# A selective-scan and expert-mixture layer: stores of the preparation in another order, square ahead of logarithm, earlier first tiles, two accumulators

## The chip, the cores and the metric

The kernel runs on one core of a Trainium2 chip. The core has five engines with a queue each: TensorE (PE; its weight loads are listed as PEld), VectorE (DVE), ScalarE (ACT), GpSimd (POOL) and SyncE (SP), which here only starts transfers. All transfers run on the core's 16 DMA engines. The metric is the device time in microseconds of one execution; the median of several runs counts.

## The reference, cut to what matters

The input is 8 batches of 512 tokens of width 128. After a layer norm, two things are added to the input: a two-way Mamba block (16 states, 256 channels, forward and backward) and a mixture of 16 experts of which each token takes 4.

```python
xn = layernorm(x)
xz = einsum('ed,bld->bel', in_proj_w, xn);  x_, z = split(xz)
# for each direction:
u = silu(causal_conv(x_, conv_w) + conv_b)              # 4 taps
x_dbl = einsum('bdl,kd->bkl', u, xproj_w)               # rank 8, B (16), C (16)
delta = softplus(dtproj_w @ x_dbl[:, :8] + dt_bias)
dA = exp(delta * A);  dBx = delta * B * u
h = scan(h = dA * h + dBx)                              # along the 512 tokens
y = (einsum('bdln,bnl->bdl', h, C) + D * u) * silu(z)
mamba = out_proj(y_forward + y_backward)
# experts:
logits = -|xn - keys|^2 + rw @ xn + rb;  top 4, softmax -> w
ffn = sum over 4 of w * (gelu(xn @ w1[e] + b1[e]) @ w2[e] + b2[e])
out = x + mamba + ffn
```

## The kernel before, in words

Everything is hand-scheduled: each engine has one program, and semaphores order them. There are three stages.

**Start (about the first 50 us).** Input and constants are loaded, the layer norm and the routing are computed, and a slot in a table sorted by expert is worked out for each of the 4096 x 4 (token, expert) pairs (`pos`, ready in two parts). SP meanwhile fills `slots_d`, the table in device memory, with rows of zeros, and `acc_d`, the accumulator in device memory, with a copy of the input.

**Preparation (one `prepare(b)` for each of 8 batches).** On each engine the batches follow one another.
- ACT: copies `xdbl` and `part1` out of PSUM (L852, L853), takes the absolute value of the delta projection (L859), loads the table of exponential and logarithm (L861), `Exp` of minus it into `mag` (L863), `part2` (L865), the skip term (L868), logarithm of 1 + `mag` (L874), square of `small` into `fit` (L876), x of batch b+2 (L832), `parts_p` (L881), another table load and SiLU of the convolution to `u` of batch b+1 (L846), SiLU of z of batch b+2 into `zg` (L837).
- DVE: the convolution of batch b+1 (`convolve`, L1371 the first tap, L1376 three more, each tap four instructions), `small` = min(`mag`, 1/32) (L1393), the polynomial from `fit` and `small` (L1398), the larger of it and the logarithm (L1404), delta (L1411), delta times u (`du_p`, L1417). L1398 waits for the square.
- SP: stores what is ready to device memory (`store_prepared`: `c_d`, skip, parts, delta, gate, du), each as soon as its turn in SP's order comes and its source is ready.
- PE: the projections; the delta projection (L1097) uses 9 rows of `xdbl` and of `dtw`.
- POOL: beside all this, 128 indirect scatters (L750, one for each 128 rows and choice k) of the normalised tokens into `slots_d`, in four rounds of 32. Ahead of each round it waits until the last one has landed and copies a column of gates (L746).

**Scan.** For each batch, 32 pairs q = 0 to 31 (16 states in twos by 4 channel blocks). For each pair PE fills PSUM with B (L1220 or L1223), DVE multiplies (`dbx`, L1467) and scans twice (L1479), ACT makes the decays (L990), POOL multiplies with C (L783; some pairs DVE, L1487), and PE sums into PSUM four pairs later (L1159, `SUM_LAG`). Rings of 8 buffers hold decays and states. Between these, a table of events lets the expert tiles of 256 rows, 10 for each batch, run beside the scan: "T" turns a tile's rows (L1173), "U0"/"U1" the first layer (L1180), "D" the second (L1188), and ACT empties each bank. For a "D" ACT scales the result into `yrows` (L936; buffer j % 2), and POOL adds it to `acc_d` with two indirect transfers (L768, `send`). Ahead of each `send`, `sums_landed` waits until the adds of both buffers have landed, that is, all tiles before. Batch 0 has a table of its own, in which its ten tiles start at the pairs `FIRST_T`:

```python
FIRST_T = [5, 7, 9, 11, 13] + T_STEP[GROUP:]
```

SP reads the first tiles' rows in `read_first`, once all scatters have landed. PE, ACT and POOL are strictly in order: a "T" that waits for its rows holds back every fill and sum behind it on PE.

**End.** After the last scan SP waits until all adds have landed, reads `acc_d` back in 8 parts, DVE adds the Mamba result to each (L1531) and SP stores it. The last batch's own output projection (L1203) is done on PE after the last scans.

## Time and profile before

| | |
|---|---|
| median of 3 runs | 1144.69 us (1136.71, 1144.69, 1153.21) |
| the profiled execution: its time | 1141.97 us |
| its span, first to last instruction | 1140.1 us |
| mean granted clock of TensorE | 0.938 |
| DVE busy | 1042.6 us, 91% of the span |
| ACT busy | 940.7 us, 83% |
| PE busy | 933.3 us, 82% |
| POOL busy | 900.5 us, 79% |
| DMA | 222.65 MB, mean 195 GB/s |

The stages lie in the profiled execution about so: start 0 to 52 us, preparation 52 to 254 us, scan 254 to 1110 us, end 1110 to 1140 us. Busy shares are an average over these. In each stage another wait decides, so the stages are read one by one.

### The profile page before, as it was taken

To read this page: it belongs to the slowest core of one execution; us is meant where nothing else is said; L and a number is where in the kernel's file an instruction comes from. 1 tells how busy PE (TensorE), PEld (TensorE's weight loads), DVE (VectorE), ACT (ScalarE), POOL (GpSimd) and SP (SyncE) were. 2 spreads that over 40 slices of the span, in tenths; PEclk is the share of its full clock that TensorE was granted. 3 is DMA by queue.
4 is the path that set the end of the run, shared out by engine and by line. 5 is a ranking of instruction groups with operands and counts; after the bars stand their busy time and mean duration, and the time that the engine had idled before them with its cause. 6 is when DMAs were issued, how large, how long until landed. Compare 5 with 4: busy or idle time off the path is not lost.

```text
span 1140.1 us, 21850 instructions
## 1 busy us (share of the span) xinstructions
PE 933.3 (82%) x5866; PEld 738.2 (65%) x5866; DVE 1042.6 (91%) x1354; ACT 940.7 (83%) x1732; POOL 900.5 (79%) x545
## 2 busy tenths in 40 slices
PE   4476886754899988999998889899999989898982
PEld 2233332323678777878877677788788778776771
DVE  7878998959999999999999999999999999896991
ACT  4258888775899999999998889999999999887920
POOL 3278778657579979998999799799989989995742
PEclk9789989775899999999999999999999999998995
DMA  9924564486666867687687668677866877764545
GB/s 312 365 102 166 203 220 183 158 327 191 231 177 167 215 196 186 180 233 193 174 218 187 181 175 238 184 184 194 224 188 172 220 202 203 170 158 124 140 111 159
DMA packets 151299, 222.65 MB, mean 195 GB/s; under 512 B 36028, under 2 KB 97756, under 8 KB 146276
## 3 DMA queue, kind: packets, MB, share of 16 engines
q1 hardware_dynamic: 124036, 202.16, 56.0%
q0 software_dynamic: 27136, 19.02, 11.7%
q8 instruction: 51, 0.84, 0.3%
q14 instruction: 76, 0.62, 0.2%
HBM read 159.74 MB, written 65.52 MB: 198 GB/s over the span
## 4 chain that ended last, share of the span: by engine, by line
issue 22%; POOL 17%; DMA 6%; PE 6%; ACT 5%; DVE 3%; SPq 2%; POOLq 0%; DVEq 0%; ACTq 0%
POOL arena L783 9%; POOL acc_d L768 8%; DMA acc_d<-yrows,tags 4%; DVE arena L1479 2%; PE ps L1188 2%; ACT arena L990 2%; DMA tags<-slots_d 1%; PE ps L1159 1%; DVE ps L1467 1%; PE ps L1220 1%; ACT arena L930 1%; ACT arena L911 1%; ACT arena L958 1%; PE ps L1180 1%; DMA arena<-acc_d 0%
## 5 line engine op out<-in xcount | busy, mean ns | idle before, releaser
L1479 DVE TENSOR_TENSOR_SCAN arena<-arena,ps 128x512 f32<-128x512 f32 x512 | 597.3, 1201 | 1.1 <-issue 1.0
L783 POOL TENSOR_TENSOR arena<-arena 128x1024 f32<-128x1024 f32 x237 | 510.1, 2455 | 68.2 <-DVE arena L1479 67.4
L990 ACT ACTIVATE arena<-delta,a_neg 128x511 f32<-128x511 f32 x512 | 340.5, 726 | 6.0 <-DVE arena L1426 3.3
L768 POOL DMA_INDIRECT acc_d<-yrows,tags x160 | 252.5, 1578 | 61.1 <-issue 36.4
L1159 PE MATMUL ps<-ident,arena 128*128 128x128 f32 x2048 | 274.1, 278 | 7.5 <-POOL arena L783 5.1
L1467 DVE TENSOR_TENSOR ps<-du,ps 128x512 f32<-128x512 f32 x352 | 232.3, 675 | 23.0 <-PE ps L1223 20.4
L1159 PEld LDWEIGHTS ps<-ident,arena 128*128 128x128 f32 x2048 | 236.4, 144 | 20.7 <-POOL arena L783 5.6
L750 POOL DMA_INDIRECT slots_d<-arena,pos x128 | 161.0, 1258 | 47.3 <-issue 44.4
L1188 PE MATMUL ps<-w,arena 128*128 128x128 f32 x1248 | 174.7, 283 | 3.5 <-ACT arena L958 2.4
L1180 PE MATMUL ps<-rowsT,w 128*128 128x256 f32 x640 | 155.8, 387 | 11.6 <-ACT arena L941 7.6
L1188 PEld LDWEIGHTS ps<-w,arena 128*128 128x128 f32 x1248 | 154.2, 192 | 14.0 <-issue 4.5
L911 ACT ACTIVATE arena<-arena 128x256 f32<-128x256 f32 x320 | 145.1, 509 | 0.0
L1180 PEld LDWEIGHTS ps<-rowsT,w 128*128 128x128 f32 x640 | 119.4, 194 | 31.4 <-ACT arena L941 9.3
L930 ACT ACTIVATE arena<-ps,w 128x256 f32<-128x256 f32 x312 | 123.8, 476 | 4.2 <-PE ps L1180 3.6
L1220 PE MATMUL ps<-ident,arena 128*128 128x128 f32 x640 | 95.3, 279 | 23.8 <-DVE arena L1479 19.6
L936 ACT ACTIVATE yrows<-ps,tags 128x128 f32<-128x128 f32 x160 | 49.8, 364 | 65.7 <-PE ps L1190 45.2
L1220 PEld LDWEIGHTS ps<-ident,arena 128*128 128x128 f32 x640 | 74.6, 144 | 29.6 <-DVE arena L1479 22.6
L958 ACT ACTIVATE arena<-arena 128x1024 f32<-128x1024 f32 x78 | 79.1, 1053 | 0.2
L1223 PE MATMUL ps<-parts,sel 128*128 128x512 bf16 x176 | 60.3, 396 | 15.2 <-DVE arena L1479 15.1
L1376 DVE SCALAR_TENSOR_TENSOR arena<-arena,chan 128x512 f32<-128x512 f32 x96 | 64.2, 740 | 0.0
L1173 PE MATMUL ps<-ident,rows 128*128 128x128 f32 x160 | 34.0, 295 | 34.9 <-DMA tags<-slots_d 16.4
L1173 PEld LDWEIGHTS ps<-ident,rows 128*128 128x128 f32 x160 | 18.0, 143 | 51.9 <-ACT arena L930 21.1
(147 smaller groups left out, 913.5 us busy)
## 6 DMA issues: line engine op xcount, KB each, us to landing
arena<-c_d SPq DMA_DIRECT2D x128, 512.0 KB, 4.2
w<-w_dram SPq DMA_DIRECT2D x80, 258.0 KB
w<-w_dram SPq DMA_DIRECT2D x80, 256.0 KB
rows<-slots_d SPq DMA_DIRECT2D x80, 130.0 KB
slots_d<-delta SPq DMA_DIRECT2D x5, 2015.0 KB, 19.2
delta_d<-arena SPq DMA_DIRECT2D x8, 1024.0 KB, 3.9
du_d<-delta SPq DMA_DIRECT2D x8, 1024.0 KB, 6.2
delta<-delta_d SPq DMA_DIRECT2D x8, 1024.0 KB, 7.4
```

The lines of the kernel that those rows point to most:

```text
L750: pool.indirect_dma_start(slots_d, bass.IndirectOffsetOnAxis(ap=pos[:, t * TOPK + k:t * TOPK + k + 1], axis=0), xn[:, t, :], None).then_in ...
L768: pool.indirect_dma_start(acc_d, bass.IndirectOffsetOnAxis(ap=tags[:, j, a, 0:1].bitcast(I32), axis=0), yrows[:, j % W_RING, a, :], None, ...
L783: nc.gpsimd.tensor_tensor(state[:, q % H_RING], state[:, q % H_RING], c_rows[:, r % C_RING], ALU.mult).then_inc(s["prod_done"], 1)
L911: last = nc.scalar.activation(scaled_du[scaled_slot(g, j)][:, t, :], duT[:, par, t, :], ACT.Identity, scale=bT[:, par, t, n:n + 1])
L930: last = nc.scalar.activation(hidden[hidden_slot(b, j)][:, c, :], bank[:, f * S:(f + 1) * S], ACT.Identity, bias=w1[:, j % W_RING, FF + c: ...
L990: nc.scalar.activation(decay[:, q % DA_RING, j, lo:lo + L - 1], delta[:, par, dh, lo:lo + L - 1], ACT.Exp, scale=a_neg[:, dh, 2 * g + j:2 ...
L1159: last = nc.tensor.matmul(y_ps[:, h, t * P:(t + 1) * P], state[:, q % H_RING, j, t * P:(t + 1) * P], ident[:, :], is_transpose=True, start ...
L1180: last = nc.tensor.matmul(bank[:, f * S:(f + 1) * S], w1[:, slot, c * P:(c + 1) * P], rowsT[:, :], start=True, stop=True)
L1188: nc.tensor.matmul(bank[:, a * P:(a + 1) * P], kept[:, c, a * P:(a + 1) * P], w2[:, slot, c, :], start=c == 0, stop=False)
L1220: last = nc.tensor.transpose(bank[:, t * P:(t + 1) * P], scaled_du[scaled_slot(g, j)][:, t, h * P:(h + 1) * P], ident[:, :])
L1467: nc.vector.tensor_tensor(b_ps[:, ROW[q, j], j, :], du[:, par, q % DH, :], b_row, ALU.mult)\
L1479: nc.vector.tensor_tensor_scan(state[:, q % H_RING, j, way], decay[:, q % DA_RING, j, way], b_ps[:, ROW[q, j], j, way], 0.0, ALU.mult, ALU ...
```

## The change

It has these parts.
1. **Square ahead of logarithm** on ACT in `prepare`, and on DVE the convolution of batch b+1 is cut for b = 1 to 6: three taps ahead of `small`, the fourth behind it. The wait for the last store of `du_p` moves from `small` to `du_p` itself.
2. **Stores**: the gate of batch b+1 is stored behind parts of batch b (before: gate of b+2, behind delta), and du of batch b behind skip of batch b+1 (before: at once).
3. **Two accumulators**: `acc_d` becomes a list of two; buffer j % 2 of `yrows` adds into its own. The second is filled with zeros by four more transfers (4.1 MB) behind the store of the first gate. `sums_landed` waits only for the adds of the same buffer. At the end both are read back and added: 16 reads and 16 additions where there were 8 and 8.
4. **First tiles**: the tiles of batch 0 start at pairs 2, 4, 7, 10, 13.
5. **Start**: 80 small matmuls on PE ahead of all others; `ones` is set by POOL; POOL also clears `dtw` and a part of `du`; the delta projection uses all 128 rows (unused ones multiply by zero); the two `drop` instructions stand ahead of the routing on DVE.

```diff
-FIRST_T = [5, 7, 9, 11, 13] + T_STEP[GROUP:]
+FIRST_T = [2, 4, 7, 10, 13] + T_STEP[GROUP:]
+WARM = 80
-        acc_d = dram("acc_d", (UNUSED + TOK, D))
+        acc_d = [dram(f"acc{i}_d", (UNUSED + TOK, D)) for i in range(W_RING)]
@@ SP, store_prepared
                 store(b, skip_d, skip_p.rearrange("p h l -> p (h l)"), "skip_sb", "skip_out")
+                if b > 0:
+                    store_du(b - 1)
                 store(b, parts_d, parts_p.rearrange("p d l -> p (d l)"), "parts_ready", "parts_out")
+                if b + 1 < BATCH:
+                    store_gate(b + 1)
                 store(b, delta_d, pos_part.rearrange("p q l -> p (q l)"), "delta_ready", "delta_out", ND)
-                if b + 2 < BATCH:
-                    store_gate(b + 2)
-                store(b, du_d, du_p.rearrange("p q l -> p (q l)"), "du_ready", "du_out", ND)
...
             store_gate(0)
-            store_gate(1)
+            sp.wait_ge(s["zero_acc"], 1)
+            for at, n in ZERO_ACC:
+                sp.dma_start(acc_d[1][at:at + P * n].rearrange("(p r) d -> p (r d)", p=P),
+                             du[:, 0, :, :].rearrange("p q l -> p (q l)")[:, 0:n * D]).then_inc(s["acc_filled"], 16)
@@ SP, end
             for i in range(W_RING):
                 sp.wait_ge(y_out[i], 16 * SH * (NTILE // W_RING))
+                for b in range(BATCH):
+                    sp.dma_start(acc[i][:, b, :], acc_d[i][UNUSED + L * b:UNUSED + L * (b + 1)].rearrange("(p t) d -> p (t d)", p=P))\
+                        .then_inc(acc_in[i][b], 16)
@@ POOL
             def sums_landed(b, before, j):
                 half = MPB // W_RING * (b - before)
-                for i in range(W_RING):
-                    wait(pool, y_out[i], 16 * SH * (half + (j + W_RING - 1 - i) // W_RING))
-                    pool.sem_inc(s["pool_step"], 1)
+                wait(pool, y_out[j % W_RING], 16 * SH * (half + j // W_RING))
+                pool.sem_inc(s["pool_step"], 1)
@@ ACT, prepare
+                act.wait_ge(s["small_ready"], b + 1)
+                nc.scalar.activation(fit, small, ACT.Square, scale=SQ_SCALE, bias=fit_bias[:, 0:1]).then_inc(s["square_ready"], 1)
                 act.wait_ge(s["exp_ready"], b + 1)
                 if b == 0:
                     act.wait_ge(s["sel_ready"], 1)
                 nc.scalar.activation(ln1p, mag, ACT.Ln, scale=LN_SCALE, bias=ln_bias[:, 0:1]).then_inc(s["ln_ready"], 1)
-                act.wait_ge(s["small_ready"], b + 1)
-                nc.scalar.activation(fit, small, ACT.Square, scale=SQ_SCALE, bias=fit_bias[:, 0:1]).then_inc(s["square_ready"], 1)
@@ PE
+            pe.wait_ge(s["ones_set"], 1)
+            for k in range(WARM):
+                nc.tensor.matmul(ps[:, 0, 0:P], ones[:, :], ones[:, :], start=True, stop=True)
...
-                        last = nc.tensor.matmul(ps[:, DT_BANK + d * NH + h, :], dtw[BR:BR + NR + 1, d, h * P:(h + 1) * P],
-                                                xdbl[BR:BR + NR + 1, d, :], start=True, stop=True)
+                        last = nc.tensor.matmul(ps[:, DT_BANK + d * NH + h, :], dtw[:, d, h * P:(h + 1) * P], xdbl[:, d, :],
+                                                start=True, stop=True)
@@ DVE, prepare
-                    convolve(b + 1)
+                    convolve(b + 1, range(KC) if b == 0 else range(KC - 1))
...
-                wait(dve, s["du_out"], 16 * b)
                 nc.vector.tensor_scalar(small, mag, SMALL, None, ALU.min).then_inc(s["small_ready"], 1)
+                if 0 < b < BATCH - 1:
+                    convolve(b + 1, range(KC - 1, KC))
```

DVE in the preparation, one batch (the convolution of the next batch, `small`, which is written into `du`, and the polynomial), before:

```order
L1371 TENSOR_SCALAR arena<-arena,chan 128x512 x4
L1376 SCALAR_TENSOR_TENSOR arena<-arena,chan 128x512 x12
L1393 TENSOR_SCALAR du<-arena 128x2048
L1398 SCALAR_TENSOR_TENSOR arena<-arena,du 128x1024 x2
L1404 SCALAR_TENSOR_TENSOR arena<-arena 128x1024 x2
```

And of the change (L1399, L1404 the convolution, L1420 `small`, L1427 the polynomial):

```order
L1399 TENSOR_SCALAR arena<-arena,chan 128x512 x4
L1404 SCALAR_TENSOR_TENSOR arena<-arena,chan 128x512 x8
L1420 TENSOR_SCALAR du<-arena 128x2048
L1404 SCALAR_TENSOR_TENSOR arena<-arena,chan 128x512 x4
L1427 SCALAR_TENSOR_TENSOR arena<-arena,du 128x1024 x2
```

Four instructions of the convolution now stand between `small` and the first reader of the square.

SP in the preparation, the stores of one batch (`w` is `zg`, the gate; `delta` is `du_p`), before:

```order
L590 DMA c_d<-arena 16x2x512
L582 DMA skip_d<-gatedT 128x1024
L582 DMA parts_d<-arena 128x1024
L582 DMA delta_d<-arena 128x2048
L582 DMA gate_d<-w 128x1024
L582 DMA du_d<-delta 128x2048
```

And of the change, for batches 1 to 6:

```order
L601 DMA c_d<-arena 16x2x512
L590 DMA skip_d<-gatedT 128x1024
L590 DMA du_d<-delta 128x2048
L590 DMA parts_d<-arena 128x1024
L590 DMA gate_d<-w 128x1024
L590 DMA delta_d<-arena 128x2048
```

Where delta, gate and du stood together, du now goes with skip, and the gate with parts.

PE at the beginning of the scan of batch 0 (L1220/L1223 fills, L1173 the "T" of a tile, L1180 its "U", L1159 sums), before:

```order
L1223 MATMUL ps<-parts,sel 128x512 x2
L1220 MATMUL ps<-ident,arena 128x128 x4
L1223 MATMUL ps<-parts,sel 128x512
L1159 MATMUL ps<-ident,arena 128x128 x8
L1220 MATMUL ps<-ident,arena 128x128 x4
L1173 MATMUL ps<-ident,rows 128x128 x2
```

And of the change (L1247/L1244 fills, L1197 "T", L1204 "U", L1183 sums):

```order
L1247 MATMUL ps<-parts,sel 128x512 x2
L1197 MATMUL ps<-ident,rows 128x128 x2
L1244 MATMUL ps<-ident,arena 128x128 x4
L1247 MATMUL ps<-parts,sel 128x512
L1204 MATMUL ps<-rowsT,w 128x256 x4
L1197 MATMUL ps<-ident,rows 128x128 x2
L1183 MATMUL ps<-ident,arena 128x128 x8
L1244 MATMUL ps<-ident,arena 128x128 x4
```

The first tile's "T" moved ahead of the fills of pair 4, and the second tile's ahead of the first sum and of the fill of pair 5.

## Rows read from the trace of the kernel before

**Rows 1.** Busy time by stretch: length, PE, PEld, DVE, ACT, POOL, clock, DMA share, GB/s.
```profile
500.00:600.00 100.00, 92.25 (x679) 80.78 (x678) 99.34 (x111) 94.22 (x192) 91.23 (x51) 1.00 0.75 198
```
**Rows 2.** Timeline of DVE, preparation: start, duration, instruction, [idle before <-releaser].
```profile
106.32 1.22 DVE L1393 TENSOR_SCALAR du<-arena 128x2048 f32<-128x2048 f32 x1
109.61 2.36 DVE L1398 SCALAR_TENSOR_TENSOR arena<-arena,du 128x1024 f32<-128x1024 f32 x2 [2.07 <-ACT arena L876]
...
120.52 8.03 DVE L1376 SCALAR_TENSOR_TENSOR arena<-arena,chan 128x512 f32<-128x512 f32 x12
128.47 1.21 DVE L1393 TENSOR_SCALAR du<-arena 128x2048 f32<-128x2048 f32 x1
```
**Rows 3.** Waits of ACT, 80 to 235 us: who for whom, total, times, longest.
```profile
ACT arena L876 <- DVE du L1393: 1.6, 3, 0.5
```
**Rows 4.** Timeline of ACT: one of these waits, SiLU of z, a wait for PE.
```profile
107.57 2.00 ACT L876 ACTIVATE arena<-du,fit_bias 128x2048 f32<-128x2048 f32 x1 [0.55 <-DVE du L1393]
...
114.60 1.01 ACT L837 ACTIVATE w<-ps 128x1024 f32<-128x1024 f32 x1
...
117.72 0.59 ACT L852 COPY arena<-ps 104x512 f32<-104x512 f32 x1 [0.60 <-PE ps L1082]
```
**Rows 5.** Issues by line: size, median us from issue to landing.
```profile
gate_d<-w SPq DMA_DIRECT2D x8, 512.0 KB, 4.8
skip_d<-gatedT SPq DMA_DIRECT2D x8, 512.0 KB, 2.7
```
**Rows 6.** Timeline of DVE: last batch of the preparation, first scan.
```profile
243.23 2.36 DVE L1398 SCALAR_TENSOR_TENSOR arena<-arena,du 128x1024 f32<-128x1024 f32 x2 [5.03 <-ACT arena L876]
...
254.48 0.69 DVE L1467 TENSOR_TENSOR ps<-du,ps 128x512 f32<-128x512 f32 x1 [1.96 <-issue]
```
**Rows 7.** Timeline of POOL: its three longest stalls among the 128 scatters, the last scatter.
```profile
98.41 9.95 POOL L750 DMA_INDIRECT slots_d<-arena,pos  x1 [0.30 <-issue]
...
214.18 4.36 POOL L746 COPY arena<-gates 128x32 f32<-128x32 f32 x1 [5.62 <-DMA slots_d<-arena,pos]
...
250.32 1.77 POOL L750 DMA_INDIRECT slots_d<-arena,pos  x1 [7.51 <-issue]
...
269.68 0.96 POOL L750 DMA_INDIRECT slots_d<-arena,pos  x1 [0.30 <-issue]
```
**Rows 8.** Timeline of SP, DVE and PE, scan of batch 0.
```profile
273.07 4.60 DVE L1487 TENSOR_TENSOR arena<-arena 128x1024 f32<-128x1024 f32 x1
273.40 0.43 SPq L548 DMA_DIRECT2D rows<-slots_d  x1
...
276.50 0.69 PE L1173 MATMUL ps<-ident,rows 128*128 128x128 f32 x2 [0.95 <-DMA tags<-slots_d]
277.38 0.44 SPq L548 DMA_DIRECT2D rows<-slots_d  x1
277.59 2.32 DVE L1479 TENSOR_TENSOR_SCAN arena<-arena,ps 128x512 f32<-128x512 f32 x2
...
295.31 1.29 DVE L1467 TENSOR_TENSOR ps<-du,ps 128x512 f32<-128x512 f32 x2 [1.79 <-PE ps L1223]
```
**Rows 9.** Timeline of all engines, the end of the kernel.
```profile
1106.83 0.62 ACT L936 ACTIVATE yrows<-ps,tags 128x128 f32<-128x128 f32 x2 [9.30 <-DMA acc_d<-yrows,tags]
...
1110.91 0.69 DVE L1453 TENSOR_TENSOR gated<-ps,gate 128x512 f32<-128x512 f32 x1 [0.59 <-PE ps L1159]
...
1116.32 3.75 PE L1203 MATMUL ps<-outw,gatedT 128*128 128x128 f32 x16 [0.77 <-ACT gatedT L939]
...
1124.76 3.67 SPq L694 DMA_DIRECT2D arena<-acc_d  x8
1127.48 1.30 DVE L1531 TENSOR_TENSOR arena<-arena,delta 128x512 f32<-128x512 f32 x2 [15.88 <-DMA arena<-acc_d]
...
1133.70 0.69 DVE L1531 TENSOR_TENSOR arena<-arena,ps 128x512 f32<-128x512 f32 x1
```
**Rows 10.** Timeline of DVE, start.
```profile
30.77 0.29 DVE L1301 TENSOR_TENSOR arena<-ps,arena 128x128 f32<-128x128 f32 x1 [1.09 <-PE ps L1040]
```

83 lines of the change are left out of this document (51 added, 32 removed).

## The prediction

> **What bounds the kernel now.** I read the stages one by one: first the busy time by stretch, then the waits and the timeline of the engine that is full in each stage, then the end. In the scan DVE is that engine: in 100 us of it DVE is busy 99.34 us [rows 1]. Nothing in the change shortens a DVE instruction there, so it can gain only where DVE stands still: in the preparation, at the entry of the scan, and at the end.
>
> In the preparation a batch takes 22.15 us, from `small` of one batch (106.32) to that of the next (128.47) [rows 2]. In it DVE idles 2.07 us, for the square, and is busy about 20.1. ACT is hardly freer: of the seven periods only three have a wait for `small`, 1.6 us in all [rows 3]; its other waits are for PE, such as 0.60 us for the projection [rows 4]. So ACT with PE's answers needs about (7 x 22.15 - 1.6) / 7 = 21.9 us a batch whatever DVE does.
>
> At the entry of the scan the scatters of POOL decide. The last is issued at 269.68 and done at 270.64 [rows 7], while DVE has scanned since 254.48 [rows 6]. The first tile's "T" runs on PE at 276.50 when its rows have landed, 5.9 us after the last scatter; DVE begins pair 5 at 277.59 [rows 8].
>
> The end is a chain through `acc_d`. DVE finishes its own work at 1111.6 (1110.91 + 0.69), yet the read of the accumulator starts at 1124.76 and the last addition at 1133.70 [rows 9]. The adds of one tile wait for those of the tile before: ACT stood 9.30 us for one such landing [rows 9].
>
> **Part 1, square and split convolution.** The square (2.00 us [rows 4]) goes ahead of the logarithm, and the fourth tap (4 of the 12 instructions that take 8.03, so 2.7 us [rows 2]) lies over it. DVE's 2.07 us of idleness vanish in each of six batches, 12.4 us of DVE time. But ACT's 21.9 us stand behind it; DVE will wait for the exponential instead. What is left is ACT's own 1.6 us. In the last batch there is no convolution to hide in, and DVE waits 5.03 us for logarithm and square in turn [rows 6]; with the square first it waits one instruction less, 1.9 us. Full rows in the delta projection may raise TensorE's clock in a few waits; I take nothing, at most 2 us. So the scan starts at 254.48 - 1.6 - 1.9 = 251.0.
>
> **Part 2, stores.** SiLU of z on ACT needs the last gate stored. It starts at 114.60; the square ends at 109.57 [rows 4], and behind it come the copies of x and of parts, 1.0 us each on ACT, so z follows the end of parts by some 3.1 us. The gate's store is now issued just behind that of parts, some 0.4 us after that end. A gate store of before lands in 4.8 us, but behind 1 MB of delta; the skip store of the same size, with nothing ahead of it, in 2.7 us [rows 5]. With 2.7 the wait is nil; with 4.8 it is 0.4 + 4.8 - 3.1 = 2.1 us, of which ACT's following waits for PE (0.60 in [rows 4], and one of about the same size ahead of it) absorb 1.1: 1.0 us in each of six batches. I take nothing and keep 6 us as the upper end. du waits for skip of the next batch and has until `du_p` is written again, some 10 us: hidden. What the other order can change is POOL. Three stalls stand out among its scatters [rows 7]: one of 9.95 us instead of 0.96, a wait of 5.62 with a copy of 4.36, and an idle time of 7.51: 26.5 us. The first two begin within 4 us of the burst delta, gate, du. The first covers the whole chain of 12 convolution instructions and `small` that DVE runs without a gap (98.4 to 107.5), and the copy ends with `small` of its batch as well. Both causes go: the burst is cut, and DVE now waits for the exponential ahead of `small`, which lets POOL in. The third falls in the reads for the first scan, which stay. I take the first two as gone: the last scatter is done at 270.64 - 9.0 - 9.98, about 252, instead of 270.6; the other end is no change.
>
> The Trainium skill, page "SBUF — State Buffer", section "SBUF: two separate sides", says that DVE and GpSimd share a port pair that is locked for a whole instruction, and that descriptors of GpSimd's transfers can't be written while DVE holds it. The copy of 4.36 us agrees with that. By this rule alone a DVE with less idle time starves POOL more, and the scatters end no earlier; that is the second rival.
>
> **Part 4, first tiles.** "T" of tile 0 now stands on PE ahead of the fills of pair 4, that of tile 1 ahead of the first sum and the fill of pair 5. With X for the end of the last scatter, tile 0's rows are there at X + 5.9. Tile 1's are asked for 4.0 us later (273.40 and 277.38 [rows 8]), so at X + 9.9; then "T" 0.7, a sum 1.9, a fill 1.1: DVE can begin pair 5 at X + 13.7. Unhindered it begins it as long after its first scan as before, less the 3.4 us by which a product (4.60 us, while POOL multiplied too; 1.2 is usual) was longer [rows 8]: 277.59 - 254.48 - 3.4 = 19.7, so 251.0 + 19.7 = 270.7. The later of the two counts; they meet at X = 257. With X = 252 DVE is at pair 5 at 270.7 instead of 277.6, 6.9 us gained, and the stall of 1.79 us at 295.31 [rows 8] goes too, since the third tile has a pair more: 8.7 us. Each microsecond of X beyond 257 is lost in full.
>
> **Part 3, two accumulators.** In the scan they bring nothing: DVE is full [rows 1]. At the end a tile's adds need only wait for the tile before the last. The last "D" is computed before 1103 and its adds would have landed by about 1112. Then DVE's own chain is the end: 7 + 8 + 1 additions of 0.69 us from 1111.6, so 1122.6, and what follows the last addition is as before (1140.1 - 1134.4 = 5.7): 1128.3, 11.8 us less. The last projection (1116.32 [rows 9], 2.7 us earlier when ACT isn't held) is ready in time. The other end: the reads are 16 now. Before, the additions came as their parts landed, 8 parts over 1127.48 to 1133.70, 0.89 us each, stores beside them [rows 9]; at that pace the sixteenth part, read from 1109.7, lands at 1125.8 and the end is 7.5 us earlier. I take 10. The zero-fill (4.1 MB from about 58 us on) lies where SP has nothing urgent: nothing.
>
> **Part 5, start.** A warm TensorE can remove at most DVE's wait of 1.09 us [rows 10]; the two `drop` instructions cost DVE what they save later. I take 0.5.
>
> **Sum.** 10 + 8.7 + 0.5 = 19.2 us; 1141.97 (the profiled execution's time) - 19.2 = 1122.8. The median shown is 2.7 above that execution; I put half of that on top: 1124.
>
> **The rivals.**
> 1. *Only one stall goes.* X = 262: pair 5 at 275.7, gain 1.9 + 1.8; total 14.2, about 1129. For it: the two stalls need not have one cause. Chance 0.20.
> 2. *POOL gains nothing* (the rule above). X = 270.6: pair 5 at 284.3, 6.7 lost, 1.8 gained; the preparation's gain is swallowed; 5.6 in all, about 1137. For it: the scatters are issued by POOL alone, and DVE is as busy. Against it: the stalls fall on bursts. Chance 0.18.
> 3. *The gate store is late.* 6 us of preparation lost, in part hidden because X decides next: about 1128. Chance 0.06.
> 4. *Reads bind the end*: 7.5 instead of 10, about 1127. Chance 0.09.
> 5. *Slower than before.* One mechanism: PE blocks at pair 2 on rows that come later than now. All gains are used up when X + 13.7 = 277.6 + 1.8 + 10 + 0.5, at X = 276; that needs scatters 5 us later than before, for instance one more stall of 9.95 us, from the 4.1 MB of zero-fill beside the first round: X = 280.6, about 1148. For it: a stall of that kind exists and its cause isn't shown; against it: the bursts shrink. Chance 0.05. Over 2% slower would need X above 299.
>
> **How the numbers follow.** The forecast (1124) has 0.42 and reaches from 1116 (11.8 at the end, 2 from the clock, half the third stall) to 1128. Rivals 1, 3 and 4 end at 1127 to 1129, rival 2 at 1137. A range of 1114 to 1138 leaves out rival 5 and the tails, less than 0.2. Within 2% (about what a measurement of this kernel can tell from no change) means 1121.8 to 1167.6: the faster part of the forecast lies below it. Faster 0.33, within 0.63, slower 0.04.
>
> **What would show it.** In the changed profile: the period of the preparation about 21.9 us, DVE idle ahead of `small` and not ahead of the polynomial; no wait of ACT ahead of SiLU of z; the last scatter near 252 and the first "T" 6 us later; DVE at pair 5 near 271; no wait of ACT for a landing after 1060, and from the last gated product to the end 17 to 21 us instead of 28.5. The prediction is wrong if the last scatter stays near 270, or if the reads at the end come as slowly as before.

## The result, and the profile of the changed kernel

The change made the kernel a little slower. The median is 1152.99 us (1147.99 to 1156.24, four runs) against 1140.7 us (1135.42 to 1153.21, four runs) of the kernel before on the same chip: ratio 1.0112, 95% interval 1.0075 to 1.0149. The prediction was 1124 us and a range of 1114 to 1138; the time lies outside, on the other side of no change.

| | before | changed |
|---|---|---|
| the profiled execution: its time | 1141.97 us | 1147.99 us |
| its span | 1140.1 us | 1146.1 us |
| mean granted clock of TensorE | 0.938 | 0.935 |
| last scatter done (X) | 270.6 us | 285.3 us |
| first `dbx` of the scan | 254.5 us | 249.6 us |
| DVE begins pair 5 | 277.6 us | 298.3 us |
| last gated product done | 1111.6 us | 1124.4 us |
| from there to the end of the span | 28.5 us | 21.7 us |

So two of the three gains came, in the preparation (4.9 us) and at the end (6.8 us), and the third place, the entry of the scan, lost 20.7 us.

Where it was lost is in the timeline of POOL, the answer to [rows 7]. Here is the last scatter and what follows it on the changed kernel (start, duration, engine, line, instruction, [idle before <-releaser]):

```profile
284.30 0.96 POOL L770 DMA_INDIRECT slots_d<-arena,pos  x1 [0.30 <-issue]
285.27 5.91 POOL L802 TENSOR_TENSOR arena<-arena 128x1024 f32<-128x1024 f32 x3
...
291.34 0.69 PE L1197 MATMUL ps<-ident,rows 128*128 128x128 f32 x2 [38.18 <-DMA tags<-slots_d]
...
293.35 0.69 DVE L1494 TENSOR_TENSOR ps<-du,ps 128x512 f32<-128x512 f32 x1 [28.15 <-PE ps L1247]
...
298.32 2.33 DVE L1506 TENSOR_TENSOR_SCAN arena<-arena,ps 128x512 f32<-128x512 f32 x2 [0.33 <-PE ps L1244]
```

PE came to the "T" of tile 0 (L1197) early, as the new `FIRST_T` wants, and stood 38.18 us for its rows. Everything behind it on PE waited, so DVE stood 28.15 us for one fill (L1247). Before, the two stalls of DVE in this place were 1.79 us and a product of 4.60 us [rows 8].

The stalls of 9.95 and 5.62 + 4.36 us [rows 7] are gone, as forecast. But the scatters as a group cost more than before: 183.2 us of POOL (128 of 1431 ns) instead of 161.0 (128 of 1258 ns). In six batches the same pattern stands in the timeline. One of them, with DVE beside it (L1420 `small`, L1404 the fourth tap, L1427 the polynomial, L1433 the maximum, L1440 delta, L1448 delta times u):

```profile
126.93 2.73 DVE L1404 SCALAR_TENSOR_TENSOR arena<-arena,chan 128x512 f32<-128x512 f32 x4
128.15 1.02 POOL L770 DMA_INDIRECT slots_d<-arena,pos  x1 [0.30 <-issue]
129.47 5.56 POOL L770 DMA_INDIRECT slots_d<-arena,pos  x1 [0.30 <-issue]
129.58 2.35 DVE L1427 SCALAR_TENSOR_TENSOR arena<-arena,du 128x1024 f32<-128x1024 f32 x2
131.85 2.35 DVE L1433 SCALAR_TENSOR_TENSOR arena<-arena 128x1024 f32<-128x1024 f32 x2
134.12 2.35 DVE L1440 SCALAR_TENSOR_TENSOR arena<-ps,arena 128x1024 f32<-128x1024 f32 x2
135.34 0.96 POOL L770 DMA_INDIRECT slots_d<-arena,pos  x1 [0.30 <-issue]
136.39 2.35 DVE L1448 TENSOR_TENSOR delta<-arena 128x1024 f32<-128x1024 f32 x2
136.60 2.96 POOL L770 DMA_INDIRECT slots_d<-arena,pos  x1 [0.30 <-issue]
```

A scatter issued 0.11 us ahead of the polynomial takes 5.56 us instead of 0.96. It ends 0.91 us after DVE has begun the first instruction that takes an input from PSUM (L1440), 0.05 less than a scatter takes alone: it begins anew, as it seems, once DVE has passed on. The next long one (2.96 us) lies over delta times u, whose inputs are both in SBUF. Before, DVE stood 2.07 us ahead of the polynomial [rows 2]; the change filled that gap with the fourth tap.

The changed kernel holds a comparison of its own. In its first batch there is no fourth tap behind `small`, so DVE stands still ahead of the polynomial, and the scatter issued 0.08 us ahead of it, almost the same moment as above, is through in 0.96 us:

```profile
84.32 0.96 POOL L770 DMA_INDIRECT slots_d<-arena,pos  x1 [0.30 <-issue]
84.40 2.36 DVE L1427 SCALAR_TENSOR_TENSOR arena<-arena,du 128x1024 f32<-128x1024 f32 x2 [2.48 <-ACT arena L892]
85.59 2.00 POOL L770 DMA_INDIRECT slots_d<-arena,pos  x1 [0.30 <-issue]
```

The gain at the end has the size of the rival "reads bind the end", but not its cause. To be held against [rows 9] (the line with x8 is from a narrower window of the same 16 reads, the last line from the view of SP's waits: total, times, longest):

```profile
1120.52 0.63 ACT L956 ACTIVATE yrows<-ps,tags 128x128 f32<-128x128 f32 x2 [7.54 <-DMA acc_d<-yrows,tags]
1121.28 12.92 SPq L710 DMA_DIRECT2D arena<-acc_d  x16
...
1123.67 0.69 DVE L1480 TENSOR_TENSOR gated<-ps,gate 128x512 f32<-128x512 f32 x1 [0.59 <-PE ps L1183]
...
1130.55 3.65 SPq L710 DMA_DIRECT2D arena<-acc_d  x8
1133.07 1.35 DVE L1559 TENSOR_TENSOR arena<-arena 128x512 f32<-128x512 f32 x2 [3.01 <-DMA arena<-acc_d]
...
1139.67 0.69 DVE L1561 TENSOR_TENSOR arena<-arena 128x512 f32<-128x512 f32 x1
...
SPq L710 <- DMA acc_d<-yrows,tags: 5.3, 1, 5.3
```

The 16 reads span 12.92 us, where 8 took 3.67, but not because SP is slow to issue them. The eight of the first accumulator begin at 1121.28; then SP waits 5.3 us for the last adds into the second one, and issues its eight from 1130.55 in 3.65 us. Those adds are late because ACT had stood 7.54 us for earlier adds of the same buffer to land before it could write the last `yrows`. The last group of reads begins 6.2 us after the last gated product, before it was 13.2 us (1124.76 against 1111.6), and from there to the end of the span it is as long as before (15.6 against 15.3 us). So the 6.8 us are the earlier landing of the last adds.

### The profile page after: what moved, and what is told of

Same layout as the page of the kernel before. It is cut to its first block, busy times and chain, and to the rows that moved or that the text cites. A ratio compares the mean times of both kernels' runs of the same rounds, so it can differ in the third digit from the quotient of the medians.

```text
span 1146.1 us, 21950 instructions
## 1 busy us (share of the span) xinstructions
PE 927.8 (81%) x5946; PEld 739.5 (65%) x5946; DVE 1042.3 (91%) x1361; ACT 939.8 (82%) x1732; POOL 922.1 (80%) x548
## 4 chain that ended last, share of the span: by engine, by line
issue 17%; POOL 13%; ACT 13%; PE 10%; DMA 4%; DVE 2%; SPq 1%; POOLq 0%; DVEq 0%; ACTq 0%
POOL arena L802 7%; POOL acc_d L787 7%; ACT arena L1010 5%; PE ps L1212 3%; PE ps L1183 2%; DMA acc_d<-yrows,tags 2%; ACT arena L931 2%; ACT arena L950 2%; DVE arena L1506 2%; PE ps L1204 1%; ACT arena L978 1%; DMA tags<-slots_d 1%; PE ps L1244 1%; ACT yrows L956 1%; PE ps L1214 1%
## 5 line engine op out<-in xcount | busy, mean ns | idle before, releaser
L787 POOL DMA_INDIRECT acc_d<-yrows,tags x160 | 253.5, 1584 | 47.6 <-issue 39.6
L1183 PE MATMUL ps<-ident,arena 128*128 128x128 f32 x2048 | 271.7, 276 | 2.4 <-DVE arena L1514 2.4
L1183 PEld LDWEIGHTS ps<-ident,arena 128*128 128x128 f32 x2048 | 234.5, 143 | 14.5 <-DVE arena L1514 2.6
L770 POOL DMA_INDIRECT slots_d<-arena,pos x128 | 183.2, 1431 | 44.6 <-issue 41.8
L1204 PE MATMUL ps<-rowsT,w 128*128 128x256 f32 x640 | 153.2, 382 | 10.4 <-ACT arena L961 7.5
L1204 PEld LDWEIGHTS ps<-rowsT,w 128*128 128x128 f32 x640 | 118.1, 191 | 29.4 <-ACT arena L961 9.0
L1244 PE MATMUL ps<-ident,arena 128*128 128x128 f32 x640 | 96.1, 280 | 20.0 <-DVE arena L1506 14.5
L1244 PEld LDWEIGHTS ps<-ident,arena 128*128 128x128 f32 x640 | 75.1, 144 | 25.9 <-DVE arena L1506 19.1
L1197 PE MATMUL ps<-ident,rows 128*128 128x128 f32 x160 | 33.6, 293 | 70.2 <-DMA tags<-slots_d 49.6
L1197 PEld LDWEIGHTS ps<-ident,rows 128*128 128x128 f32 x160 | 18.1, 142 | 86.3 <-DMA tags<-slots_d 46.7
L1247 PE MATMUL ps<-parts,sel 128*128 128x512 bf16 x176 | 59.0, 390 | 14.0 <-DVE arena L1506 13.9
L1404 DVE SCALAR_TENSOR_TENSOR arena<-arena,chan 128x512 f32<-128x512 f32 x96 | 64.7, 742 | 0.0
```

Source lines behind the costliest of these rows:

```text
L770: pool.indirect_dma_start(slots_d, bass.IndirectOffsetOnAxis(ap=pos[:, t * TOPK + k:t * TOPK + k + 1], axis=0), xn[:, t, :], None).then_in ...
L787: pool.indirect_dma_start(acc_d[j % W_RING], bass.IndirectOffsetOnAxis(ap=tags[:, j, a, 0:1].bitcast(I32), axis=0), yrows[:, j % W_RING, a ...
L1183: last = nc.tensor.matmul(y_ps[:, h, t * P:(t + 1) * P], state[:, q % H_RING, j, t * P:(t + 1) * P], ident[:, :], is_transpose=True, start ...
L1204: last = nc.tensor.matmul(bank[:, f * S:(f + 1) * S], w1[:, slot, c * P:(c + 1) * P], rowsT[:, :], start=True, stop=True)
L1244: last = nc.tensor.transpose(bank[:, t * P:(t + 1) * P], scaled_du[scaled_slot(g, j)][:, t, h * P:(h + 1) * P], ident[:, :])
```

## The experiments

The theory after reading the trace, G below: the fourth tap fills DVE's gap; with it gone, DVE's unbroken chain of instructions with both inputs in SBUF holds POOL's scatters back; and the early "T" on PE turns each microsecond of the late scatters into a stall of DVE. The rivals: the zero-fill of 4.1 MB (Z) or the new order of the stores (S) delays the scatters; the early tiles are slow by themselves (F). "Time" is always the ratio to the kernel before, measured beside it.

### Tiles at pair five, whole convolution, both

The first undoes part 4 in the changed kernel:

```diff
-FIRST_T = [2, 4, 7, 10, 13] + T_STEP[GROUP:]
+FIRST_T = [5, 7, 9, 11, 13] + T_STEP[GROUP:]
```

> The changed kernel with FIRST_T at 5, 7, 9, 11, 13 again, all else kept. Theory G (the filled gap on DVE holds POOL's scatters back, and the early first tiles make PE stand for them): the scatters don't move, last one done at about 285; DVE comes to pair 5 at about X + 6 to X + 8, so 291 to 293 instead of 298.3, some 5 to 7 us earlier, and of these some 3 to 6 are left at the end: about 1143 to 1146 in the place of 1148 to 1153. Rival F (the early tiles alone make the change slow, the late scatters would be harmless without them): DVE at pair 5 near 278 and the time 12 us or more below the changed kernel, ahead of before by the 7 us of the end. Rival Z (the 4.1 MB of zero-fill delay the scatters): last scatter at 285, as G has it.

Measured: ratio 1.005 (1.0017 to 1.0083), last scatter done at 283.3. DVE comes to pair 5 at X + 5.0:

```profile
282.39 0.96 POOL L770 DMA_INDIRECT slots_d<-arena,pos  x1 [0.30 <-issue]
288.37 2.33 DVE L1506 TENSOR_TENSOR_SCAN arena<-arena,ps 128x512 f32<-128x512 f32 x2 [19.81 <-PE ps L1244]
```

The early tiles account for some 0.6% of the 1.1% (a difference of two ratios whose intervals overlap), and the late scatters hurt without them too. F falls as the sole cause.

The second puts the fourth tap back, ahead of `small`:

```diff
-                    convolve(b + 1, range(KC) if b == 0 else range(KC - 1))
+                    convolve(b + 1, range(KC))
...
-                if 0 < b < BATCH - 1:
-                    convolve(b + 1, range(KC - 1, KC))
```

> The changed kernel with the convolution whole again ahead of small (all four taps), square first, new stores, tiles at pair 2. Theory G: DVE again waits some 2 us for the square in each batch, POOL gets its descriptors written in that gap, the six scatters of 5.56 us shrink to about 2, the last scatter is done between 255 and 270; DVE at pair 5 at X + 13.7, so 271 to 284; the preparation itself ends about 4 us later (first dbx near 253 to 254). Time 8 to 20 us below the changed kernel. Rival Z (zero-fill) and rival S (the new order of the stores delays the scatters): last scatter near 285 still, time within 3 us of the changed kernel or slower by the longer preparation.

Measured: ratio 0.9912 (0.9864 to 0.9961), 1134.46 us. No scatter over 2.5 us is left, the last is done at 260.5, 24.8 us earlier:

```profile
259.54 0.96 POOL L770 DMA_INDIRECT slots_d<-arena,pos  x1 [0.30 <-issue]
```

DVE is at pair 5 at 277.1. Zero-fill and new stores are all in this kernel, so Z and S fall: moving four instructions of 0.68 us in each of six batches turns a kernel 1.1% slower than before into one 0.9% faster.

The third does both.

> The changed kernel with both: convolution whole ahead of small, tiles at 5, 7, 9, 11, 13. What stays of the change is square first, the new stores, two accumulators and the start. Theory G: last scatter as in the kernel with the whole convolution (255 to 270), DVE at pair 5 at 274 to 278 whatever it is, the end 7 us shorter than before: about 1130 to 1136, below both kernels. Rivals Z and S: last scatter near 285, pair 5 near 291, about 1145.

Measured: ratio 0.9896 (0.9848 to 0.9945), 1131.95 us; last scatter done at 262.8, pair 5 at 276.3. With the scatters on time it can't be told from the second kernel: once X is near 260, these runs show neither help nor harm from the early tiles.

### The gap without the moved work

If the fourth tap is left out in the batches 2 to 7, DVE stands still in its place (the kernel then leaves out part of the convolution, so only its times are of use):

```diff
                 if 0 < b < BATCH - 1:
-                    convolve(b + 1, range(KC - 1, KC))
+                    dve.wait_ge(s["v_chain"], start + (KC - 1) * DH * (b + 2))
+                    dve.sem_inc(s["v_ready"], 1)
```

> The changed kernel without the fourth tap of the convolution in the batches 2 to 7 (four DVE instructions of 0.69 us each left out in each of six batches, so the convolution has three taps there); all else is kept, the order and the waits too. DVE is idle for some 2 us between small and the polynomial, as before the change. Theory G (what holds the scatters is DVE's unbroken chain of fourth tap and polynomial): the six scatters of 5.56 us are gone, the longest ones in a batch are below 3.5 us, last scatter done 15 to 25 us earlier, at 260 to 270. Rivals Z and S (zero-fill, stores): the scatters of 5.56 us stay in the same places of the batch, last scatter near 285 less only the 0 to 3 us by which DVE has less to do.

Measured: ratio 0.9902 (0.9867 to 0.9937), last scatter done at 259.4, first `dbx` at 248.8. The same place in a batch:

```profile
104.87 2.36 DVE L1428 SCALAR_TENSOR_TENSOR arena<-arena,du 128x1024 f32<-128x1024 f32 x2 [2.48 <-ACT arena L892]
106.06 2.01 POOL L770 DMA_INDIRECT slots_d<-arena,pos  x1 [0.30 <-issue]
107.15 2.35 DVE L1434 SCALAR_TENSOR_TENSOR arena<-arena 128x1024 f32<-128x1024 f32 x2
108.37 1.97 POOL L770 DMA_INDIRECT slots_d<-arena,pos  x1 [0.30 <-issue]
```

With the gap back, two scatters get through under the same four wide instructions that held one for 5.56 us. The batch is as short as in the changed kernel (21.87 us both, over five batches). So the length of the batch isn't what matters, but that DVE's chain is broken just ahead of them. Here DVE also has less to do; the whole convolution above and the tiny copies below keep all its work and agree.

### Short instructions

Polynomial and maximum in pieces of 512 elements, in the changed kernel:

```diff
-                    nc.vector.scalar_tensor_tensor(fit[:, way], fit[:, way], SQ_REST, small[:, way], ALU.add, ALU.mult)\
-                        .then_inc(s["fit_ready"], 1)
+                    for q in range(d * NH, (d + 1) * NH):
+                        last = nc.vector.scalar_tensor_tensor(fit[:, q], fit[:, q], SQ_REST, small[:, q], ALU.add, ALU.mult)
+                    last.then_inc(s["fit_ready"], 1)
```

(and the maximum in the same way)

> The changed kernel with the two wide pairs behind the fourth tap (polynomial and maximum) cut into instructions of 512 elements: eight of about 0.68 us in the place of four of 1.18, so 0.9 us more for DVE a batch, which it has. The filled gap stays filled. Theory G, narrow form (POOL gets in between short instructions, as it does in the chain of taps, and not between the wide ones): the 5.56 us scatters shrink to 1 to 2 us, last scatter near 262, time 8 to 15 us below the changed kernel. Wide form (what counts is only that DVE's chain is unbroken from before the scatter on, however short its instructions): the scatters of 5.56 us become 6 to 7 us, last scatter at 285 to 290, time as the changed kernel.

Measured: ratio 1.0094 (1.0063 to 1.0125), last scatter done at 285.9. The wide form holds:

```profile
129.49 5.83 POOL L770 DMA_INDIRECT slots_d<-arena,pos  x1 [0.30 <-issue]
129.60 2.49 DVE L1428 SCALAR_TENSOR_TENSOR arena<-arena,du 128x512 f32<-128x512 f32 x4
132.01 2.48 DVE L1435 SCALAR_TENSOR_TENSOR arena<-arena 128x512 f32<-128x512 f32 x4
```

The chain is 0.27 us longer and so is the scatter: shorter instructions don't free a scatter that is held. Where DVE stands still ahead of the polynomial, in the first batch, they do matter. There a scatter passes beneath the halves at full pace, while beneath the wide ones of the changed kernel it took 2.00 us (85.59 above):

```profile
85.49 0.96 POOL L770 DMA_INDIRECT slots_d<-arena,pos  x1 [0.31 <-issue]
```

### A tiny instruction in the chain

The changed kernel with two copies of 16 columns, out of PSUM:

```diff
                     dve.wait_ge(s["small_ready"], b + 1)
+                    if d == 0:
+                        dve.wait_ge(s["dt_ps"], ND * b + ND)
+                        nc.vector.tensor_copy(gap[:, :], ps[:, DT_BANK, 0:16])
                     nc.vector.scalar_tensor_tensor(fit...
```

(the same ahead of the maximum; `...` stands for the unchanged arguments)

> The changed kernel with two tiny DVE instructions more in each batch: a copy of 16 columns out of PSUM ahead of the polynomial and one ahead of the maximum. If DVE's wide instructions that take both inputs from SBUF hold POOL back and any short instruction that leaves the shared side alone lets it in, the scatters of 5.56 us become 2 to 3.3 us, the last one is done at 262 to 272 and the time is 8 to 15 us below the changed kernel. If only a stretch in which DVE stands still, or reads PSUM for about a microsecond, lets POOL in: 5.56 becomes 5.7 to 6, last scatter near 285, time as the changed kernel.

Measured: ratio 0.996 (0.9924 to 0.9995), last scatter done at 268.6.

```profile
128.53 1.02 POOL L771 DMA_INDIRECT slots_d<-arena,pos  x1 [0.30 <-issue]
128.63 0.17 DVE L1430 COPY gap<-ps 128x16 f32<-128x16 f32 x1
128.72 2.35 DVE L1431 SCALAR_TENSOR_TENSOR arena<-arena,du 128x1024 f32<-128x1024 f32 x2
129.85 2.04 POOL L771 DMA_INDIRECT slots_d<-arena,pos  x1 [0.30 <-issue]
130.99 0.17 DVE L1439 COPY gap<-ps 128x16 f32<-128x16 f32 x1
131.07 2.35 DVE L1440 SCALAR_TENSOR_TENSOR arena<-arena 128x1024 f32<-128x1024 f32 x2
132.20 2.05 POOL L771 DMA_INDIRECT slots_d<-arena,pos  x1 [0.30 <-issue]
```

The scatter issued 0.10 us ahead of the tiny copy is through in 1.02 us. Then the same with the copy out of SBUF:

> The same as the run before it (e11), but the two tiny instructions copy 16 values a partition from SBUF (the constants of the channels) instead of from PSUM. If reading PSUM is what frees POOL, the 5.56 us scatters stay here and go in e11; if an instruction with one input is enough, both let POOL in; if the moment at which the scatter meets DVE's instructions decides, either may shift it by its 0.1 us and the two runs need not agree with either rule.

Measured: ratio 0.998 (0.9947 to 1.0013), last scatter done at 264.7 (the profiled execution took 1145.79 us, the longest of the ten).

```profile
127.12 1.04 POOL L771 DMA_INDIRECT slots_d<-arena,pos  x1 [0.30 <-issue]
127.23 0.17 DVE L1429 COPY gap<-chan 128x16 f32<-128x16 f32 x1
127.31 2.35 DVE L1430 SCALAR_TENSOR_TENSOR arena<-arena,du 128x1024 f32<-128x1024 f32 x2
128.46 2.05 POOL L771 DMA_INDIRECT slots_d<-arena,pos  x1 [0.30 <-issue]
```

One input from SBUF is as good as one from PSUM: 0.17 us in the right place take 4.5 us off the scatter that was held. It need not be an input from PSUM. But not every instruction with a single input does it: the scatter of 9.95 us [rows 7] was held through `small` as well, and was done 0.82 us after `small` had ended (106.32 + 1.22 [rows 2]), not 0.9 us after it began.

### Single parts on the kernel before

First tiles alone (`FIRST_T` as in the change):

> The kernel before with the first tiles at pairs 2, 4, 7, 10, 13 and nothing else. My theory of the entry (PE stands for the rows, DVE comes to pair 5 at X + 13.7, X the end of the last scatter): X as before, near 270.6, pair 5 near 284.3 instead of 277.6, 6.7 us lost there; the later stall of 1.79 goes, and part of the rest is given back in the last batches: 0 to 5 us slower than before. Rival (the order of the first tiles costs nothing by itself): pair 5 near 278, the time as before within 1 us.

Measured: ratio 1.0036 (1.0002 to 1.0071), X = 270.7, DVE at pair 5 at 283.65 (X + 13.0). The prediction's working for the entry of the scan holds.

Two accumulators alone (zero-fill, `sums_landed`, reads and additions of part 3):

> The kernel before with the two accumulators alone (with the 4.1 MB of zero-fill behind the first two gate stores, 16 reads and 16 additions at the end). Reads bind the end: from the last gated product to the end about 21.7 us as in the changed kernel, 6.8 less than the 28.5 of before, time 5 to 8 us below before. If the zero-fill delays the scatters (rival Z): last scatter 5 us or more behind 270.6, and the gain is eaten at the entry of the scan. If the second accumulator helped in the scan too: more than 8 us.

Measured: ratio 0.9947 (0.9917 to 0.9977), so some 6 us; X = 268.4, earlier than before and not later, with a stall of 9.95 us in the old place. From the last gated product (done at 1111.4) to the end of the span (1133.1) are 21.7 us, as in the changed kernel. The reads are the same as there, 12.98 us with a wait of 5.4 us for the last adds between the two groups. Part 3 is worth 6.8 us at the end, nothing in the scan, and its zero-fill costs the scatters nothing.

The old order of the stores in the kernel with the whole convolution:

```diff
                 store(b, delta_d, pos_part.rearrange("p q l -> p (q l)"), "delta_ready", "delta_out", ND)
+                if b + 2 < BATCH:
+                    store_gate(b + 2)
+                store_du(b)
...
```

(The new places of both stores are taken out, and the second gate is stored at the start again.)

> As the kernel with the whole convolution and the tiles at pair 2 (e2), but with the stores in the order of before (gate of b+2 behind delta, then du at once). If the bursts of stores made POOL's stalls, as the prediction has it: a stall of 4 us or more is back and the last scatter is done at 268 to 272, 8 to 12 us later than the 260.5 of e2; time 3 to 8 us above e2. If the order of the stores does nothing to POOL (only the length of DVE's unbroken chains and where they meet a scatter does): last scatter at 258 to 264 and the time within 3 us of e2.

Measured: ratio 0.9937 (0.9899 to 0.9975), X = 265.2, 4.7 us later than with the new stores (one profile each; the two kernels with the whole convolution and the new stores, whose preparation is the same, differ by 2.3 us in X themselves); the time can't be told from theirs. The stall of 9.95 us does not come back, a wait with a long copy ahead of a round does:

```profile
211.59 4.45 POOL L765 COPY arena<-gates 128x32 f32<-128x32 f32 x1 [5.53 <-DMA slots_d<-arena,pos]
```

So the old order of the stores does not by itself bring the 9.95 us, against what the prediction took, and the 4.45 us are not bound to it either: a copy of 4.00 us stands in the kernel without the fourth tap, with the new stores.

Part 1 alone:

```diff
                 nc.vector.tensor_scalar(small, mag, SMALL, None, ALU.min).then_inc(s["small_ready"], 1)
+                if 0 < b < BATCH - 1:
+                    convolve(b + 1, range(KC - 1, KC))
...
```

(and the square ahead of the logarithm on ACT)

> The kernel before with part 1 alone: square ahead of logarithm on ACT and the fourth tap behind small (stores, first tiles, one accumulator and start as before). Theory G: the scatters of 5.6 to 5.8 us are there, one in each of six batches, last scatter done at 283 to 288 instead of 270.6; first scan some 4 us earlier (250 to 251); with the first tiles at pair 5 DVE comes to that pair at X + 4 to X + 6, so 288 to 292, 11 to 14 us later than before, and the time is 5 to 10 us above before. Rival S (the new order of the stores is needed for the late scatters): last scatter near 270, time 3 to 5 us below before.

Measured: ratio 0.9996 (0.9961 to 1.0032). Here theory G missed: no scatter over 2.5 us, the last done at 253.6. But the batches took 23.64 us (five from 103.80 to 222.01), DVE stood ahead of the polynomial again, and the first `dbx` came at 261.7 instead of 250. What went with it is in the windows (length, PE, PEld, DVE, ACT, POOL, clock, DMA share, GB/s):

```profile
150.00:175.00 25.00, 21.59 (x43) 9.44 (x42) 20.68 (x26) 20.40 (x20) 18.78 (x18) 0.77 0.50 182
```

TensorE was granted 0.77 of its clock there (a mix of its two levels, 1.2 and 2.4 GHz), ACT waited for it, 12.1 us for the delta projection and 9.2 us for the skip term over the preparation, where the kernel before has 11.3 and 1.3. The gap that the tap had filled opened again, for another reason. What was then open is which other part of the change gives the short batch; two runs tell it.

Parts 1 and 5 on the kernel before (the edit above with the 80 matmuls, the cleared `dtw` and the full rows):

> The kernel before with parts 1 and 5 (square first, fourth tap behind small; start and delta projection over all 128 rows), with the stores, tiles and accumulator of before. With part 1 alone (e10) TensorE was granted 0.77 to 0.80 through the preparation, a batch took some 23.7 us, DVE stood 0.5 to 1.5 us ahead of the polynomial, and no scatter was long. If the full rows are what keeps the clock up: clock 0.86 to 1.0 there, a batch 21.3 to 22 us, and then theory G: the 5.56 us scatters are there, last scatter at 280 to 286, time 4 to 9 us above before. If the new order of the stores is what made the short batch of the changed kernel: a batch stays near 23.7, last scatter near 255, time as before.

Measured: ratio 1.0122 (1.0049 to 1.0195), not to be told from the whole change. The long scatters are back in five of the six batches, three of 5.56 us and two of 4.90:

```profile
127.15 5.56 POOL L754 DMA_INDIRECT slots_d<-arena,pos  x1 [0.30 <-issue]
...
149.03 2.36 DVE L1412 SCALAR_TENSOR_TENSOR arena<-arena,du 128x1024 f32<-128x1024 f32 x2
149.59 4.90 POOL L754 DMA_INDIRECT slots_d<-arena,pos  x1 [0.30 <-issue]
...
170.40 2.35 DVE L1412 SCALAR_TENSOR_TENSOR arena<-arena,du 128x1024 f32<-128x1024 f32 x2
170.98 1.47 POOL L754 DMA_INDIRECT slots_d<-arena,pos  x1 [0.30 <-issue]
...
283.00 0.95 POOL L754 DMA_INDIRECT slots_d<-arena,pos  x1 [0.30 <-issue]
...
288.97 2.33 DVE L1491 TENSOR_TENSOR_SCAN arena<-arena,ps 128x512 f32<-128x512 f32 x2 [18.46 <-PE ps L1229]
```

In the sixth batch the scatter passed: issued 0.58 us behind the start of the polynomial, it took 1.47 us, where one issued 0.56 us behind took 4.90. The gap was filled in both. So the filled gap makes the long scatters possible, and by itself it doesn't bring one every time.

In the windows of its preparation from 100 us on the clock is 1.00, 0.89, 0.84, 0.92 and 0.77, and a batch takes 21.88 us.

And the full rows taken out of the changed kernel:

```diff
-dtw[:, d, h * P:(h + 1) * P], xdbl[:, d, :],
+dtw[BR:BR + NR + 1, d, h * P:(h + 1) * P], xdbl[BR:BR + NR + 1, d, :],
```

> The changed kernel with the delta projection over 9 rows again (all else kept, the stores too). If the full rows keep the clock up: granted clock 0.77 to 0.80 in the preparation, batches near 23.7 us, DVE stands ahead of the polynomial, no scatter of 5.56 us, last scatter at 253 to 258, first scan near 262, time 4 to 10 us below the changed kernel. If the rows do nothing: everything as in the changed kernel, last scatter at 285.

Measured: ratio 0.9999 (0.9967 to 1.0032), so 1.1% better than the changed kernel; batches of 23.65 us, the last scatter done at 257.3, the first `dbx` at 263.2, pair 5 at 283.6.

```profile
150.00:175.00 25.00, 21.59 (x42) 9.21 (x41) 20.35 (x26) 20.40 (x20) 19.20 (x16) 0.77 0.49 180
```

The two runs agree: parts 1 and 5 together are the harm. With nine rows the clock is 0.75 to 0.80 from 100 us on, PE is slow, ACT late, DVE has gaps and POOL is free; with all rows the clock is up, the batch is 1.8 us shorter, DVE has no gap behind the fourth tap, and POOL is starved. That the rows decide is shown by the last run; the steps between, from the clock to DVE's gap, are read from the waits, and no run moved the clock by itself.

### A version that beats both

The changed kernel with tiny copies out of SBUF ahead of polynomial, maximum and delta times u, and the first tiles at pair 5:

> A version meant to beat both: the changed kernel with the tiny copies out of SBUF ahead of the polynomial and of the maximum (as e12) and a third one ahead of delta times u, and with the tiles at 5, 7, 9, 11, 13. Theory G: neither the 5.56 nor the 2.96 us scatters, last scatter at 255 to 262; the filled gap stays, so the first scan is at 249; DVE at pair 5 at 268 to 272 instead of 277.6; with the 7 us of the end: 1125 to 1131. If short instructions only move the stall elsewhere: last scatter above 265 and 1134 or more.

Measured: 1130.77 us, ratio 0.9902 (0.9866 to 0.9939). First `dbx` at 251.1, last scatter done at 266.9 (later than expected), pair 5 at 273.9, 3.7 us earlier than before. The third copy bought nothing:

```profile
114.81 0.16 DVE L1453 COPY gap<-chan 128x16 f32<-128x16 f32 x1
114.88 2.35 DVE L1454 TENSOR_TENSOR delta<-arena 128x1024 f32<-128x1024 f32 x2
115.02 3.04 POOL L771 DMA_INDIRECT slots_d<-arena,pos  x1 [0.30 <-issue]
```

Here the copy came before the scatter was issued, and not behind it, which may be why. This kernel and the simpler one with the whole convolution and the tiles at pair 5 (0.9896) can't be told apart, nor from the whole convolution with the early tiles (0.9912); all are about 1% faster than before.

The runs side by side (us; batch is the mean over five; the kernels by their change):

| kernel | batch | last scatter done | first `dbx` | pair 5 | ratio to before |
|---|---|---|---|---|---|
| before | 22.2 | 270.6 | 254.5 | 277.6 | 1 |
| changed | 21.9 | 285.3 | 249.6 | 298.3 | 1.0112 |
| changed, tiles at pair 5 | 21.8 | 283.3 | 247.9 | 288.4 | 1.005 |
| changed, polynomial in halves | 21.9 | 285.9 | 249.8 | 299.1 | 1.0094 |
| parts 1 and 5 alone | 21.9 | 284.0 | 249.9 | 289.0 | 1.0122 |
| part 1 alone | 23.6 | 253.6 | 261.7 | 280.0 | 0.9996 |
| changed, nine rows | 23.6 | 257.3 | 263.2 | 283.6 | 0.9999 |
| changed, no fourth tap | 21.9 | 259.4 | 248.8 | 275.2 | 0.9902 |
| changed, whole convolution | 22.3 | 260.5 | 252.8 | 277.1 | 0.9912 |
| the same, tiles at pair 5 | 22.5 | 262.8 | 256.4 | 276.3 | 0.9896 |
| changed, tiny copies, tiles at 5 | 21.8 | 266.9 | 251.1 | 273.9 | 0.9902 |

## Why the prediction was wrong

**The failed step** is in part 2: "DVE now waits for the exponential ahead of `small`, which lets POOL in", and with it X = 252. The two stalls did vanish, but I had counted only what goes. The new place of the idle time was worked out rightly (DVE waits 1.1 to 3.5 us ahead of `small`), and I took any idle time as good for POOL. It is not: ahead of `small` the scatters ran at 0.96 to 1.02 us anyway, and the gap that was filled had been the one that broke the chain ahead of four wide instructions. Six scatters of 5.56 us and six of 2.96 us, instead of 0.96, are 6 x 4.60 + 6 x 2.00 = 39.6 us; the runs without the fourth tap (X = 259.4) and with the whole convolution (260.5) show that filling the gap, with everything else of the change in place, moves the last scatter by some 25 us.

**The rival that came true** was number 5 in its mechanism on PE and in its size: break-even at X = 276, and X above it. Its trigger was wrong: the zero-fill is innocent (X = 268.4 with it alone). Rival 2 had the right cause, that a DVE with less idle time starves POOL. But I priced it as "no gain" where it was a loss of 14.7 us. Had I put X at 285 into my own formula, I would have had pair 5 at 299.0; it came at 298.3. With that row, the 10 of the end at 6.8, the sum is 1141.97 + 20.7 - 6.8 = 1155.9; the profiled execution took 1147.99, as 7.9 of the 20.7 us were given back later in the scan (the last gated product is 12.8 us late). Of these, 4.7 us are less standing of DVE from pair 5 to the last gated product (23.3 instead of 28.0 us), the rest less busy time in that stretch (802.8 instead of 806.0).

**Part 1** (scan starts at 251.0): it started at 249.6. A batch took 21.87 us, forecast 21.9. That batch, though, rests on part 5, which I took as nothing (at most 2 us): without the full rows it is 23.6 us. I had read ACT's pace from a trace in which TensorE's clock was 0.86 to 1.0 and took that clock for granted.

**Part 2, the gate's store**: taken as nothing, and ACT stood 1.9 us for it in all over six batches, the longest 0.7: close to nothing. That bursts of stores cause POOL's stalls was argued from their being near in time. The old order with the whole convolution moves X by 4.7 us and brings no 9.95 us; as the main cause it falls. What made the stall of 9.95 us stays open.

**Part 4**: "T" at X + 5.9 and pair 5 at X + 13.7 were right (6.1 and 13.1; 13.0 with the tiles alone). The third tile did wait for its rows again, 3.22 us on PE. Even at X = 260.5 the early tiles brought nothing measurable: pair 5 came at 277.1, 2.9 us behind the formula. What those 2.9 us are was not tested, nor whether the 6.9 us are to be had at X = 252: no run with the early tiles came there.

**Part 3**: 10 us taken, 6.8 measured, both in the whole change and alone. The wrong term is that the last adds would have landed by about 1112, 0.4 us after the last gated product, so that DVE's own chain of additions binds. The reads that wait for them began 6.2 us after it, and a wait of ACT for a landing (7.54 us at 1120.52), whose absence I had named as a sign, was still there. Rival 4 comes near in size (7.5 us), but by another way: it counted 16 reads one behind the other from 1109.7, a time that no row gives, while the runs show two groups of eight with a wait for adds between them.

**Part 5**: no gain shown at the start: `small` of batch 0 comes at 80.70 against 81.44, and at 80.65 with part 1 alone. Its full rows are the hidden half of the harm.

The Trainium skill, page "SBUF — State Buffer", section "SBUF: two separate sides", calls the port pair of DVE and GpSimd an exclusive lock and says that descriptors of GpSimd's transfers can't be written while DVE holds it; it names for this DVE's instructions in a two-port mode, and those with two inputs in SBUF only against a GpSimd operation that reads SBUF. The runs agree with a lock and go beyond its wording: instructions of DVE with two fp32 inputs in SBUF hold a scatter not for one instruction but for four or eight in a row (5.56 and 5.83 us), and one of 0.17 us with a single input, placed behind the scatter's issue, ends that. Of the two readings that I weighed in the prediction, the rule was the better one, and I gave it 0.18.

What stays open is why scatters pass freely (1.02 us each) beneath the chain of taps in most batches, while one, issued 0.05 us behind the start of such a chain, was held for all twelve taps and `small` [rows 7]. In the run with parts 1 and 5, two scatters issued 0.56 and 0.58 us behind the start of the polynomial took 4.90 and 1.47 us. The moment of issue against DVE's instruction borders may decide; no run varied it by itself. It doesn't explain the effect of the gap away: with the scatter issued 0.08 to 0.11 us ahead of the polynomial, the changed kernel shows 0.96 and 0.98 us with the gap and 5.56 without.

## What to carry to other kernels

Before filling an idle gap of VectorE, look at what GpSimd does there: indirect transfers that GpSimd issues may live on just that gap, and the place of a gap counts more than its length. Where a consumer is moved earlier, work out its price at the worst time of what it waits for and not at the hoped-for one. An edit priced at nothing because its engine isn't the bound (the full rows) can still decide how the others meet. A merged line of transfers (16 in 12.92 us) can hide a wait: look at a narrower window before reading it as a pace.

## What the runs showed of the hardware

- A scatter of 128 rows issued by GpSimd takes 0.96 us and 0.30 us until the next; held back by DVE it ended 0.91 us after DVE began an instruction with an input from PSUM, or 0.82 us after the end of `small`. A copy of 16 columns (0.17 us) issued 0.10 us behind the scatter and ahead of the wide instructions turned 5.56 us into 1.02; the two scatters behind it took 2.05 each.
- The delta projection over 128 rows, with zeros in all but nine, went with a granted clock of 0.82 to 1.00 from 75 to 225 us of the changed kernel (0.77 in the window after it), the one over nine rows in the same order of work with 0.75 to 0.80 from 100 us on, and batches 1.8 us longer. The kernel before, with nine rows and the square behind the logarithm, had 0.86 to 1.00 from 75 to 200 us and 0.77 behind it: the rows alone don't set it.
- Two groups of eight reads of 256 KB took 3.99 and 3.65 us to issue, as the eight before the change did (3.67); what stretched the 16 to 12.92 us was a wait of 5.3 us for adds between them.
